# A fused cross-attention network on one core: value products of the first attention in groups of four key tiles, with six places for the probabilities

## What is computed

```python
qn = layernorm(x, ln_q_g, ln_q_b)
q = qn @ Wq * scale
kv = media @ Wkv
k, v = jnp.split(kv, 2, axis=-1)
q, k, v = (split_heads(q), split_heads(k), split_heads(v))
sim = jnp.einsum('bhid,bhjd->bhij', q, k)
sim = jnp.where(media_mask[:, None, None, :], sim, neg_inf)
attn = jax.nn.softmax(sim, axis=-1)
out = jnp.einsum('bhij,bhjd->bhid', attn, v)
out = out.transpose(0, 2, 1, 3).reshape(x.shape[0], x.shape[1], INNER)
attn_out = out @ Wo
x = x + jnp.tanh(attn_gate) * attn_out
```

## Time and profile before

| | |
|---|---|
| median of three runs | 2308.95 us (2303.93 to 2312.57) |
| profiled execution, its own time | 2304.52 us |
| its span | 2302.7 us |
| mean granted TensorE clock | 0.921 of full speed |
| busy: TensorE matmul, weight loads, VectorE, ScalarE, GpSimd | 2004.1, 1485.0, 1298.0, 923.0, 766.9 us |
| `probs` Exp on ScalarE (line 657), mean | 596 ns, 416 times |
| `prob_sums` additions on GpSimd (line 555), mean | 1289 ns, 352 times |

### The profile page before, as it was taken

How to read it: one execution, slowest core, us unless ns; L and a number is a source line. 1 busy time by engine, 2 the same in 40 slices (tenths; PEclk the granted TensorE clock), 3 DMA queues, 4 the chain that set the end, 5 groups by cost and what they waited for, 6 DMA issues and landing times.

```text
span 2302.7 us, 30843 instructions
## 1 busy us (share of the span) xinstructions
PE 2004.1 (87%) x11940; PEld 1485.0 (64%) x11940; DVE 1298.0 (56%) x2045; ACT 923.0 (40%) x1718; POOL 766.9 (33%) x676
## 2 busy tenths in 40 slices
PE   3999888898899978899889988889888998888986
PEld 2676667556677657655676766765577765775655
DVE  5666335664676623675576753367457664346733
ACT  1455232371355413257045541326415553231731
POOL 3678410000378731000237881100025886100000
PEclk9999999799899999879999998988999999887998
DMA  4000200201000020100100001020010001102000
GB/s 177 9 11 5 112 1 1 83 1 43 29 12 8 12 104 1 42 41 1 48 26 14 8 37 76 1 83 1 23 36 20 10 8 69 44 1 82 1 1 5
DMA packets 18145, 74.16 MB, mean 32 GB/s; under 512 B 2896, under 2 KB 10320, under 8 KB 14544
## 3 DMA queue, kind: packets, MB, share of 16 engines
q1 hardware_dynamic: 17424, 69.56, 8.2%
q10 hardware_dynamic: 576, 2.62, 0.3%
HBM read 71.13 MB, written 1.05 MB: 31 GB/s over the span
## 4 chain that ended last, share of the span: by engine, by line
PE 68%; DVE 17%; ACT 7%; issue 5%; POOL 2%; DMA 1%; SPq 0%; ACTq 0%; POOLq 0%; DVEq 0%
PE x L841 27%; PE pv L841 18%; PE st L841 15%; PE mi L841 6%; DVE k_hi_lo L1459 3%; ACT k_hi_lo L612 2%; DVE max_parts L1540 2%; POOL prob_sums L555 1%; ACT probs L657 1%; DVE q_lo_shift L1549 1%; DVE prob_sums L1847 1%; PE x L965 1%; DVE x_normed L1640 1%; DVE w_pair_lo L1459 1%; ACT ck_stack L745 1%
## 5 line engine op out<-in xcount | busy, mean ns | idle before, releaser
L555 POOL TENSOR_TENSOR prob_sums<-prob_sums,probs 128x512 f32<-128x512 f32 x352 | 453.6, 1289 | 65.0 <-ACT probs L657 19.0
L657 ACT ACTIVATE probs<-st 128x512 f32<-128x512 f32 x416 | 228.5, 596 | 294.4 <-PE st L841 290.8
L1540 DVE TENSOR_REDUCE max_parts<-x 128x1 f32<-128x832 f32 x256 | 250.7, 1020 | 128.6 <-PE x L841 127.4
L539 POOL TENSOR_TENSOR rstd_work<-rstd_work 128x2 f32<-128x2 f32 x24 | 16.7, 695 | 796.4 <-DVE rstd_work L1456 796.4
L1876 DVE TENSOR_REDUCE max_cross<-x 128x1 f32<-128x512 f32 x384 | 238.8, 684 | 72.0 <-PE x L841 70.5
L841 PE MATMUL st<-q_hi_hi,k_hi_lo 128*128 128x256 f32 x832 | 231.2, 309 | 17.6 <-DVE q_lo_shift L1549 17.6
L841 PE MATMUL pv<-probs,v 128*64 128x256 f32 x1664 | 231.6, 397 | 3.7 <-DVE recip_sum L1664 3.7
L841 PEld LDWEIGHTS st<-q_hi_hi,k_hi_lo 128*128 128x128 f32 x832 | 159.9, 192 | 95.5 <-issue 86.2
L841 PE MATMUL st<-q_lo_shift,k_hi_rows 128*128 128x256 f32 x832 | 210.8, 285 | 0.0
L841 PE MATMUL x<-ck_stack,cq_blocks 128*128 128x512 f32 (+1 forms) x512 | 196.4, 458 | 0.1
L841 PEld LDWEIGHTS st<-q_lo_shift,k_hi_rows 128*128 128x128 f32 x832 | 160.7, 193 | 0.1
(11 more groups left out here) (291 smaller groups left out, 4158.0 us busy)
## 6 DMA issues: line engine op xcount, KB each, us to landing
w_gate_up<-in_wgu SPq DMA_DIRECT2D x4, 3072.0 KB, 10.1
w_ff<-in_w SPq DMA_DIRECT2D x8, 1024.0 KB, 5.7
w_qk<-in_wqk SPq DMA_DIRECT2D x4, 2048.0 KB, 9.0
w_pair<-in_w SPq DMA_DIRECT2D x32, 192.0 KB, 2.3
w_down<-in_wdn SPq DMA_DIRECT2D x4, 1536.0 KB, 13.4
w_dense<-in_wd SPq DMA_DIRECT2D x4, 1024.0 KB, 12.2
mask_ints<-in_mask SPq DMA_DIRECT2D x4, 832.0 KB, 4.3
ctx_t_raw<-in_ctxT SPq DMA_DIRECT2D x4, 832.0 KB, 5.3
```

Of the source, the lines that this page charges most:

```text
L555: pool.tensor_tensor(acc[:, 0], acc[:, 0], prob[:, kt % 4], ALU.add).then_inc(add_pool.handle, 1)
L657: act.activation(prob[:, kt % 4], ST[kt % 2][:], ACT.Exp, scale=HD0 ** -0.5).then_inc(p_exp.handle, 1)
L1540: dve.tensor_reduce(mxs[:, qt, h, half:half + 1], X[n % 2][:].rearrange("p (c n) -> p c n", c=2)[:, :, 0:QUART], AX.XY, ALU.max).then_inc( ...
```

## The change

Two things are edited. The probabilities get six places: the four of `prob`, and the buffers `xa` and `xn` (`x_a` and `x_normed` in the rows), which hold 128 x 512 numbers each and are idle in the first attention. The places turn on over the pairs (tile kt of pair p is number 13p + kt, modulo six) and do not start again at each pair. So the Exp of tile kt waits for the value product and the addition of tile kt-6, and at the start of a pair for those of tiles 7 and on of the pair before. And TensorE does the value products of four key tiles at a time, in steps 4, 8 and 12, where it did those of two tiles in steps 2, 4, 6, 8, 10 and 12. The product of the last tile stays at the end of the pair.

```diff
--- before.py
+++ after.py
@@ -32,6 +32,7 @@
 LAST = S2 - (KT - 1) * P
 H0, HD0 = 16, 64
 PAIRS = H0 // 2
+SLOTS = 6
 DUOS = PAIRS // 2
 VT = -(-KT // 2)
 VS = 4
@@ -380,6 +381,11 @@

             return (ST[0][:], ST[1][:], half_bank(3))[n % 3]

+        def slot0(p, kt):
+
+            n = (p * KT + kt) % SLOTS
+            return prob[:, n] if n < 4 else (xa, xn)[n - 4][:].rearrange("p t d -> p (t d)")
+
         def slot(n):

             return prob[:, n % 8] if n % 8 < 4 else prob2[:, n % 8 - 4]
@@ -545,14 +551,14 @@
                         pool.wait_ge(p_exp.handle, p_exp.at(i, kt + 1))
                         if n == 0:
                             pool.wait_ge(sum_mm.handle, sum_mm.at(i, 0))
-                            pool.tensor_tensor(acc[:, 0], prob[:, 0], prob[:, 1], ALU.add).then_inc(add_pool.handle, 1)
+                            pool.tensor_tensor(acc[:, 0], slot0(p, 0), slot0(p, 1), ALU.add).then_inc(add_pool.handle, 1)
                             if p < PAIRS - 1:
                                 pool.wait_ge(add_pool.handle, add_pool.at(i, 1))
                                 queries(i + 1, 1 - p % 2)
                                 keys(i + 1, 1 - p % 2, 0)
                         else:
                             pool.wait_ge(add_pool.handle, add_pool.at(i, n))
-                            pool.tensor_tensor(acc[:, 0], acc[:, 0], prob[:, kt % 4], ALU.add).then_inc(add_pool.handle, 1)
+                            pool.tensor_tensor(acc[:, 0], acc[:, 0], slot0(p, kt), ALU.add).then_inc(add_pool.handle, 1)
                         if kt == 3 and p < PAIRS - 1:
                             pool.wait_ge(add_pool.handle, add_pool.at(i, n + 1))
                             keys(i + 1, 1 - p % 2, 1)
@@ -648,13 +654,16 @@

                     def probs(kt):
                         act.wait_ge(st_mm.handle, st_mm.at(i, kt + 1))
-                        if kt < 4:
+                        if kt >= SLOTS:
+                            act.wait_ge(pv_mm.handle, pv_mm.at(i, kt + 1 - SLOTS))
+                            act.wait_ge(add_pool.handle, add_pool.at(i, summed(kt - SLOTS)))
+                        elif p:
+                            act.wait_ge(pv_mm.handle, pv_mm.at(i - 1, KT + kt + 1 - SLOTS))
+                            act.wait_ge(add_pool.handle, add_pool.at(i - 1, KT + kt - SLOTS))
+                        else:
                             act.wait_ge(pv_mm.handle, pv_mm.at(i, 0))
                             act.wait_ge(add_pool.handle, add_pool.at(i, 0))
-                        else:
-                            act.wait_ge(pv_mm.handle, pv_mm.at(i, kt - 3))
-                            act.wait_ge(add_pool.handle, add_pool.at(i, summed(kt - 4)))
-                        act.activation(prob[:, kt % 4], ST[kt % 2][:], ACT.Exp, scale=HD0 ** -0.5).then_inc(p_exp.handle, 1)
+                        act.activation(slot0(p, kt), ST[kt % 2][:], ACT.Exp, scale=HD0 ** -0.5).then_inc(p_exp.handle, 1)

                     for k0 in range(0, KT, 2):
                         for kt in range(k0, min(k0 + 2, KT)):
@@ -994,7 +1003,7 @@
                             pe.wait_ge(v_read.handle, v_read.at(b * DUOS + p // 2))
                         for h in range(2):
                             r, c = slice(64 * h, 64 * h + 64), s * P + 64 * h
-                            m = mm(PV[r, 0:NT], par[p // 2 % 2]["v"][:, kt, c:c + 64], prob[:, kt % 4, h * NT:(h + 1) * NT], kt == 0, kt == KT - 1)
+                            m = mm(PV[r, 0:NT], par[p // 2 % 2]["v"][:, kt, c:c + 64], slot0(p, kt)[:, h * NT:(h + 1) * NT], kt == 0, kt == KT - 1)
                         m.then_inc(pv_mm.handle, 1)

                     pe.wait_ge(k_one.handle, k_one.at(i))
@@ -1025,9 +1034,9 @@
                             if 4 <= k0 < 12:
                                 max_part(i + 1, 1 - s, k0 - 4)
                                 max_part(i + 1, 1 - s, k0 - 3)
-                        if k0:
-                            pv(k0 - 2)
-                            pv(k0 - 1)
+                        if k0 and k0 % 4 == 0:
+                            for kt in range(k0 - 4, k0):
+                                pv(kt)
                     if p < PAIRS - 1:
                         if v_tile(p, 2):
                             d, c = v_tile(p, 2)
```

## The result

The changed kernel takes 2325.56 us in the median of six runs (2321.01 to 2335.7), beside 2308.17 us for the kernel before in six runs (2303.93 to 2313.19). The ratio is 1.0083, 95% interval 1.0065 to 1.0101: slower by 0.8%, 17 us in the medians. The profiled executions differ by a little more, 2326.78 to 2304.52 us (22.3 us): that of the kernel before lies 3.7 us under its median, that of the changed kernel 1.2 us over it. The prediction was 2322 us.

A forecast was written before the change was run, and what follows sets the result against it. The prediction took TensorE, busy 87% of the span, as the bound, with mid-pair waits set by a chain through ScalarE. Order 12 us plus clock 1.5 us put 13.5 on a median of 2309: 2322 us, range 2306 to 2346.

The forecast's parts named there:

- The main step: Steps 2 to 4: moving tiles 0 and 1 turns 1.2 us of work under a wait into idle time.
- first rival: All seven pairs of four sequences keep the full saving of 1.05 us each: 29 us less, 2280 us; chance 0.10.
- The visit: Each visit of TensorE to the value products costs 0.35 us beyond its work; three fewer save 1.05 us a pair.
- The wait in step 8: Part 5 of the maximum waits for VectorE's reduction of part 3: 0.65 us in the second, fourth, sixth and seventh pair.
- The end of a pair: From the transpose of the maximum on: second, fourth and sixth pair end 0.57 us late, first, third and fifth 0.2.
- worst case: At the pair's end `w_pair_lo` takes 1.55 us and VectorE sets the end: pairs 1.2 and 0.8 us late, +27 us.
- The eighth: Eighth pair, bound by GpSimd's additions: the Exp of tile 4 comes sooner, 0.14 us less.
- 12 us: Sum of the pairs' delays before any clock loss: 3.0 us later in a sequence, 12 us for four.
- one such drop in all: New idle time in the first six pairs brings one drop of TensorE's clock in the whole run, 1.5 us.
- The rival in which the clock drops in most pairs: Drops of 1.55 us in half or all of 24 first pairs, on top of 12: 2340 to 2358 us; chance 0.15.

The follow-up runs named there:

- four places: The kernel before with only the order of value products changed (four tiles in steps 4, 8 and 12), its four places kept: 2331.62 us, ratio 1.0106.
- the group ahead in step 8: The changed kernel with the products of tiles 4 to 7 moved right behind scores 8 and 9 in step 8: 2336.18 us, ratio 1.0123.

## Why the prediction was right

*Where the time is lost.* The main step was that value products of tiles 0 and 1 were work under a wait and that nothing up to the second part of the maximum moves. It held in the pairs from the second on and in the first of sequence 0: the idle time ahead of the value tile grew by 1.21 us to 1.44 (1.2 of work were to leave it), the second part of the maximum comes 10.6 us behind the pair's first scores (100.36 - 89.78; 100.51 - 89.94 before), and the kernel that takes away only this cover is slower still. The kernel that fills the same wait with the group is 1.2% faster than before. So the saving of visits is real and it was the place of one group that ate it. In the first pairs of the other three sequences it did not hold. All rows came from sequence 0, and these pairs have their long wait in step 2. Where 0.2 us more was said they are 1.04 to 1.16 shorter; in sequence 1, where tiles 0 and 1 covered no wait and the clock drops in both kernels, that is the first rival's 1.05.

*The visit.* 0.35 us was worked out from four rows. One of them was misread: the `pv` of 0.58 us at 215.37 is the product of `sums` (the timeline has it as `pv<-prob_sums,const_f` at 215.30), of the same shape as a value product of one tile. The price held all the same: a group of four takes 1.88 us for 1.87, and two visits fewer gave 0.7 us in the mean of the pairs, in the run with groups of two, four, two and four.

*The wait in step 8.* It appears in the second pair and not in the third. From parts 2 and 3 (104.20) part 5 (106.79) was to come 2.68 us later and came 2.59. Moved to step 10 it costs 0.6 us in the third and fifth pair, for 0.65.

*The end of a pair.* `w_pair_lo` takes 0.86 and 0.87 us in the second and third pair, from timelines of VectorE, so its worst case stayed away, and these pairs are longer by 0.54 and 0.17 us for 0.57 and 0.2:

```profile
112.95 0.86 DVE L1468 TENSOR_TENSOR w_pair_lo<-w_pair,w_pair_hi 128x384 fp32r<-128x384 f32 x1
...
138.44 0.87 DVE L1468 TENSOR_TENSOR w_pair_lo<-w_pair,w_pair_hi 128x384 fp32r<-128x384 f32 x1
```

The seventh pair, with the clock held up, is 24.70 for 23.91: 0.79 for 0.85. The eighth of sequence 0 is 0.1 shorter for 0.14. By these, order costs 3 x 0.52 + 2 x 0.16 + 0.79 - 0.1 = 2.6 us in a sequence from the second pair on, 10.4 for four. The first pairs, which I gave 0.2 each, got shorter: by 0.65 us in sequence 0, where less of the pair has the low clock, and 4.0 in all, order and clock together. So 12 us stand against 10.4 - 4.0 = 6.4.

*The clock was mis-sized.* "I add one such drop in all, 1.5 us" is the term that was off. The profiled execution has three drops in the first six pairs (27.11, 27.09, 26.67: 1.6 us each; the drops of first pairs behind their wait of about 3 us, which went from three to one, aside) and one in every seventh pair, three of which cost 2.9 us (27.55 for 24.70) and one 1.6. That is 15 us (14.3 by the sums with the idle time filled), of which the kernel before has 3.1: 11 to 12, not 1.5. I had looked at the first six pairs, where the new idle time is, and taken the seventh as it was. There 0.70 us of idle time, ahead of scores 4 and of the first part of the maximum, joined the 2.12 that were there, and with it the drop came in every place. And the drop is longer: at 233 us, 5 us behind the wait, the clock is still 0.50. The rival in which the clock drops in most pairs was wrong in its place and right in its kind: it had a drop in half or all of 24 pairs, the first six of each sequence, and the new idle time brought 3 drops behind 21 waits of 1.44 us, and the seventh pairs, which it left out, went from 2 of 4 to 4 of 4. The rule of the Trainium skill beside it (TensorE: Matmul & The Clock Gate, HAM oscillation), that each wait of a loop throttles anew, fits the seventh pairs and not the first six. That 12 + 1.5 lies near the 17 us between the medians is in part luck. The terms of the profiled executions are about 11 of order and 11 of clock from the second to the eighth pair, 4.0 less in the first pairs and 4.2 more outside of the stage, 22.3 in all; the term of the clock was too small by 10 us, and nothing stood for the last two.

*The first rival*, all savings in full, was wrong for this kernel by the place of a group and by the clock. With the group moved into the wait the time is 2277 us, near the 2280 that the rival gave, though by another sum: it has three visits fewer and the two tiles moved forward, and each pair ends on GpSimd's additions.

What stays open: why the low clock of the seventh pair lasts longer in three of four sequences after the change. The idle time ahead of it and the group of four behind it are not enough: both stand in the kernels with four places, with only the cover taken away and with the group ahead in step 8, where the seventh pair takes 26.2 to 26.6 us in ten of twelve places and 27.6 in two. All five long ones begin 0.5 to 0.7 us before the wait ends, the eleven short ones at most 0.2 us before it or later; what sets that, no run tells. Nor does one tell why everything outside of the stage takes 4.2 us more. The pairs with a single wait of 1.44 us drop in some sequences and not in others; that this hangs on when the wait comes was not tested.

## What to carry over

A short wait on an engine's row can hide long work: before moving a block, look at what would be waited for if it weren't there, not at how long the wait is now. Grouping saves 0.35 us a visit, and where each group goes decides whether the kernel keeps it: first fill the waits that an outside chain sets, then put a group between any two steps that wait for the same other engine. When TensorE gets new idle time near an old wait, price the clock at both. Look at the same pair of every sequence before multiplying by four: here the first pairs of three had another wait. And measure a gain between marks that the edit doesn't move.

## What the runs showed of the hardware

- A drop of the clock that cost 1.55 us in the seventh pair before costs 2.9 after, in three sequences of four. The chain of the changed kernel's seventh pair, where the rule is 1.88 and 1.15:

```profile
229.16 3.61 PE pv L850 x16
232.77 1.83 PE st L850 x8
```

- Ten or fifteen matmuls that nobody reads, put into waits of 1.44 and 2.12 us, kept the full clock from the second to the seventh pair of all four sequences and cost nothing on the path there. In a first pair without that wait the ten cost 1.2 us.
- Behind a single wait of 1.44 us TensorE kept the full clock in 18 of 21 places. Behind one of 2.12 us it kept it in 8 of 12, and with 0.36 and 0.33 us more of idle time just ahead in none of 16.
